# First recurrent step of a fused macaron network: the initial-state products taken out of the gates and added to their biases, and small tables copied by GpSimd

## What is computed

```python
c0 = jnp.broadcast_to(in_c, (batch, in_c.shape[0]))       # one vector, the same for every row
def step(c, xt):                                          # 4 steps over rows of 1024 x 256
    ft = sigmoid(xt @ wf.T + c @ uf.T + bf)
    it = sigmoid(xt @ wi.T + c @ ui.T + bi)
    gt = tanh(xt @ wc.T + c @ uc.T + bc)
    c = ft * c + it * gt
    return (c, None)
c_final, _ = lax.scan(step, c0, x)
h = tanh(einsum('tbi,oi->tbo', x, wo) + c_final @ uo.T + bo)
x = x + 0.5 * h
```

## Time and profile before

| | |
|---|---|
| median of 3 runs | 1934.23 us (1933.54 to 1936.37) |
| the profiled execution's own time | 1933.88 us |
| its span | 1932.1 us |
| TensorE busy | 1752.0 us (91% of the span) |
| VectorE, ScalarE, GpSimd busy | 1340.6, 1130.9, 901.4 us |
| mean granted clock of TensorE | 0.979 of 2.4 GHz |

### The profile page before, as it was taken

The page is one execution under the profiler, slowest core; times in us unless marked ns, Lnnn a source line. Parts: engine busy times, 40 slices in busy tenths (PEclk is TensorE's granted clock), DMA queues, the critical chain, the costliest instruction groups (busy, mean ns, idle before and its releaser), DMA issues. The chain is left out here.

```text
span 1932.1 us, 30828 instructions
## 1 busy us (share of the span) xinstructions
PE 1752.0 (91%) x9742; PEld 1156.5 (60%) x9742; DVE 1340.6 (69%) x2878; ACT 1130.9 (59%) x1624; POOL 901.4 (47%) x654
## 2 busy tenths in 40 slices
PE   5999787999999999997999799997898899989998
PEld 4888673222222222227888677776676676767776
DVE  4545895777777777775555588885677777768886
ACT  3323588999999999994333222213777777622220
POOL 0001116999999999994002232211554445521111
PEclk9999898999999999998999999998999999999999
DMA  4000165534535435300000000001322222300000
GB/s 152 1 0 11 65 186 103 83 44 62 69 43 72 58 46 83 45 1 12 1 0 21 23 17 0 0 0 33 125 89 88 88 88 88 121 2 22 22 21 23
DMA packets 57640, 96.96 MB, mean 50 GB/s; under 512 B 7936, under 2 KB 29664, under 8 KB 57568
## 3 DMA queue, kind: packets, MB, share of 16 engines
q1 hardware_dynamic: 55392, 94.50, 21.7%
q10 hardware_dynamic: 2176, 1.55, 0.2%
HBM read 78.98 MB, written 17.04 MB: 50 GB/s over the span
## 5 line engine op out<-in xcount | busy, mean ns | idle before, releaser
L1232 POOL TENSOR_TENSOR att_weights<-att_weights 128x1024 f32<-128x1024 f32 x288 | 541.0, 1893 | 17.7 <-DVE att_weights L1176 7.3
L1176 DVE SCALAR_TENSOR_TENSOR att_weights<-att_weights,ps 128x512 f32<-128x512 f32 x576 | 370.1, 684 | 152.3 <-ACT att_weights L1152 150.5
L1152 ACT ACTIVATE att_weights<-att_weights 128x1024 f32<-128x1024 f32 x288 | 302.5, 1051 | 0.0
L1148 ACT ACTIVATE att_weights<-ps 128x1024 f32<-128x1024 f32 x288 | 294.1, 1022 | 9.9 <-PE ps L1094 5.6
L720 DVE SCALAR_TENSOR_TENSOR X<-ps,moe_gsel,X 128x256 f32 (+1 forms) x512 | 246.6, 484 | 64.4 <-PE ps L47 48.4
L1108 PE MATMUL ps<-att_weights,att_v_ones 128*32 128x512 f32 (+3 forms) x1536 | 288.8, 497 | 2.6 <-POOL att_weights L1232 2.5
L47 PE MATMUL ps<-w_experts_hi,moe_xh 128*128 128x512 f32 x512 | 205.2, 401 | 0.0
L47 PE MATMUL ps<-w_experts_hi,moe_xl 128*128 128x512 f32 x512 | 203.1, 397 | 0.0
L47 PE MATMUL ps<-w_experts_lo,moe_xh 128*128 128x512 f32 x512 | 201.6, 394 | 0.0
L313 ACT ACTIVATE ffn_gates<-ps,ffn_gate_bias 128x512 f32<-128x512 f32 x96 | 66.1, 688 | 207.2 <-PE ps L47 200.8
L1091 PE MATMUL ps<-q_stack,k_stack 128*128 128x512 bf16 (+3 forms) x384 | 116.8, 341 | 29.5 <-DVE att_weights L1176 19.8
(11 more groups left out here) (257 smaller groups left out, 3881.4 us busy)
## 6 DMA issues: line engine op xcount, KB each, us to landing
ssm_lb<-decays SPq DMA_DIRECT2D x32, 512.0 KB, 4.5
ssm_rise<-decays SPq DMA_DIRECT2D x32, 512.0 KB, 3.8
qk_parts<-qkv_part SPq DMA_DIRECT2D x32, 384.0 KB, 2.6
q_stack<-qk_parts SPq DMA_DIRECT2D x64, 128.0 KB, 4.5
k_stack<-qk_parts SPq DMA_DIRECT2D x64, 128.0 KB, 8.2
att_q_stack<-qk_parts SPq DMA_DIRECT2D x64, 128.0 KB, 4.6
att_k_stack<-qk_parts SPq DMA_DIRECT2D x64, 128.0 KB, 8.0
out<-X SPq DMA_DIRECT2D x8, 512.0 KB, 2.9
```

The costliest lines, as they stand in the source:

```text
L1148: act.activation(Wt[:, u % WU], scores(u), ACT.Exp).then_inc(exp_done, 1)
L1152: act.activation(Wt[:, u % WU], Wt[:, u % WU], ACT.Ln, bias=1.0).then_inc(ln_done, 1)
L1176: dve.scalar_tensor_tensor(out=wt[:, t], in0=wt[:, t], scalar=LIMIT, in1=scores(u)[:, t], op0=ALU.min, op1=ALU.max).then_inc(max_done, 1)
L1232: pool.tensor_tensor(Wt[:, u % WU], Wt[:, u % WU], Wt[:, u % WU], ALU.mult).then_inc(sq_pool, 1)
```

## The change

In the first step of both feed-forward stages the units 0 to 5 hold only W times x, six matmuls instead of twelve. The products U times `in_c` are made once, in the first feed-forward stage, as six columns of PSUM: `start_products(m)` issues for each of three gates four matmuls with one moving column, in full fp32, twelve for each block. VectorE adds the gate biases to the sums (`first_bias`), and ScalarE uses that vector as the bias of its activations in the first step. The second stage uses the same vector again. In the first step the state update is `c = f * in_c + g_in` with `in_c` as a per-partition scalar, one instruction instead of two. `c`, `ch` and `cl` are no longer filled at the start, and the first step is written out ahead of the loop, which now runs over steps 1 and 2. In the first feed-forward stage the matmuls of the identity are gone, and the start products stand on both sides of the first transposes; in the second stage they stay.

In the loading stage, the load of x is issued after three small tables instead of after all nine, and the copies of small tables and the bias subtraction go from VectorE to GpSimd.

```diff
-            norm.pe_first_turn(pe, norm.var_done, ring[:, 0, 0:P], 6, 5)
+            def start_products(m):
+                for gate in range(3):
+                    col = gate * KC + m
+                    for q in range(2 * KC):
+                        part, k = (wh, wl)[q % 2], q // 2
+                        ins = pe.matmul(start_sums[:, col:col + 1], f32(part[:, 3 + gate, k, m * P:(m + 1) * P]),
+                                        in_c[:, k:k + 1], start=q == 0, stop=q == 2 * KC - 1)
+                ins.then_inc(sums_done, 1)
...
-                        matmul3(pe, out, w(wh, gate), w(wl, gate), xh, xl, range(KC), last=False)
-                        pe.wait_ge(c_split, n + 1)
-                        matmul3(pe, out, w(wh, 3 + gate), w(wl, 3 + gate), lambda k: ch[:, h, k, :],
-                                lambda k: cl[:, h, k, :], range(KC), first=False).then_inc(unit_done, 1)
+                        if first:
+                            matmul3(pe, out, w(wh, gate), w(wl, gate), xh, xl, range(KC)).then_inc(unit_done, 1)
+                        else:
+                            matmul3(pe, out, w(wh, gate), w(wl, gate), xh, xl, range(KC), last=False)
+                            pe.wait_ge(c_split, n - 1)
+                            matmul3(pe, out, w(wh, 3 + gate), w(wl, 3 + gate), lambda k: ch[:, h, k, :],
+                                    lambda k: cl[:, h, k, :], range(KC), first=False).then_inc(unit_done, 1)
...
+            if first_of_all:
+                start_products(0)
+                norm.pe_turn(pe, 0, 0)
+                start_products(1)
+            else:
+                norm.pe_first_turn(pe, norm.var_done, ring[:, 0, 0:P], 6, 5)
+            step(0, first=True)
+            with pe.Fori(1, B - 1) as i:
+                step(i)
+            step(B - 1, last=True)
...
         def _(act):
-            for h in range(HALVES):
-                for k in range(KC):
-                    ins = act.activation(c[:, h, k], in_c[:, k:k + 1].broadcast_to([P, GN]), ACT.Copy)
-            ins.then_inc(c_done, 1)
-            for h in range(HALVES):
-                for k in range(KC):
-                    ins = act.activation(ch[:, h, k], in_c[:, k:k + 1].broadcast_to([P, GN]), ACT.Copy)
-            ins.then_inc(ch_done, 1)
...
         def _(dve):
             norm.dve_stats(dve, 0, 0, lambda j: tile_of(0, 0, j))
             norm.dve_apply(dve, 0, 0, lambda j: tile_of(0, 0, j))
-            dve.wait_ge(c_done, 1)
-            dve.wait_ge(ch_done, 1)
-            dve.tensor_tensor(cl[:, :, :, :], c[:, :, :, :], f32(ch[:, :, :, :]), ALU.subtract).then_inc(c_split, 2)
             norm.dve_lo(dve, 0, 0)
+            if first_of_all:
+                dve.wait_ge(sums_done, KC)
+                dve.tensor_tensor(first_bias[:, :], start_sums, gate_bias[:, :], ALU.add).then_inc(first_done, 1)
+
+            def first_update(n, h, m):
+                f, g_in, g = (gates[:, m, q] for q in range(3))
+                dve.wait_ge(unit_read, RING + n * UNITS + 3 * m + 3)
+                dve.tensor_tensor(g_in, g_in, g, ALU.mult).then_inc(ig_done, 1)
+                dve.wait_ge(ig_done, 2 * n + m + 1)
+                dve.scalar_tensor_tensor(out=c[:, h, m], in0=f, scalar=in_c[:, m:m + 1], in1=g_in,
+                                         op0=ALU.mult, op1=ALU.add).then_inc(c_done, 1)
...
         def _(act):
+            for dst, src in smalls[:3]:
+                act.dma_start(dst, src).then_inc(small_in, 16)
+            act.dma_start(x_tiles[:, 0], batches(x_dram)[:, 0]).then_inc(x_in, 16)
+            for dst, src in smalls[3:]:
+                act.dma_start(dst, src).then_inc(small_in, 16)
             act.dma_start(mask[:, :], mask_src).then_inc(small_in, 16)
             act.dma_start(bias_raw[:, :], bias_src).then_inc(small_in, 16)
-            for dst, src in smalls:
-                act.dma_start(dst, src).then_inc(small_in, 16)
-            act.dma_start(x_tiles[:, 0], batches(x_dram)[:, 0]).then_inc(x_in, 16)
...
         def _(dve):
-            dve.wait_ge(small_in, 16 * (len(smalls) + 2))
-            dve.tensor_copy(neg[:, :], mask[:, :]).then_inc(consts_done, 1)
-            dve.tensor_copy(ident16[:, :], smalls[0][0]).then_inc(consts_done, 1)
-            dve.tensor_copy(bias3[:, :], bias_raw[:, :]).then_inc(consts_done, 1)
             split.split_lo(dve)
-            dve.wait_ge(consts_done, 3)
+        def _(pool):
+            pool.wait_ge(small_in, 16 * (len(smalls) + 2))
+            pool.tensor_copy(neg[:, :], mask[:, :])
+            pool.tensor_copy(ident16[:, :], smalls[0][0])
+            pool.tensor_copy(bias3[:, :], bias_raw[:, :]).then_inc(consts_done, 1)
+            pool.wait_ge(consts_done, 1)
             last = slice((TERMS - 1) * ROWS, TERMS * ROWS)
-            dve.tensor_tensor(bias3[last, :], bias_raw[last, :], f32(bias3[last, :]), ALU.subtract).then_inc(consts_done, 1)
-            dve.wait_ge(consts_done, 4)
+            pool.tensor_tensor(bias3[last, :], bias_raw[last, :], f32(bias3[last, :]), ALU.subtract).then_inc(consts_done, 1)
+            pool.wait_ge(consts_done, 2)
```

More of the change, by code:

```diff
@@ L215, in ffn_phase @@
     wh, wl = (part.rearrange("p (m k) c -> p m k c", k=KC) for part in W)
-    gate_bias, in_c, bo_rows = small
+    gate_bias, first_bias, in_c, bo_rows = small
     HALVES = T // GN
     UNITS = 8
+    first_of_all = x_dram is not None
     with Phase(nc) as ctx:
@@ L228, in ffn_phase @@
         ring = ps[:, 2:2 + RING]
+        start_sums = ps[:, 6, 0:3 * KC]
+        sums_done = sem(f"{tag}_sums_done")
+        first_done = sem(f"{tag}_first_done")
         unit_done = sem(f"{tag}_unit_done")
@@ L246, in _, with step @@
         def _(pe):
-            norm.pe_first_turn(pe, norm.var_done, ring[:, 0, 0:P], 6, 5)
-            def step(i, last):
+            def start_products(m):
[6 more added lines that the diff above has]
+                ins.then_inc(sums_done, 1)
+            def step(i, first=False, last=False):
                 for h in range(HALVES):
@@ L303, in _, with step @@
             norm.act_hi(act, 0, 0)
-            def step(i, last):
+            def step(i, first=False, last=False):
+                bias = first_bias if first else gate_bias
                 for h in range(HALVES):
@@ L309, in step @@
                         m, gate = u // 3, u % 3
-                        if u == 0 or u == 3:
-                            act.wait_ge(c_done, 2 * n + 1)
+                        if not first and (u == 0 or u == 3):
+                            act.wait_ge(c_done, 2 * n)
+                        if first and h and (u == 0 or u == 3):
+                            act.wait_ge(c_done, 2)
                         act.wait_ge(unit_done, n * UNITS + u + 1)
                         act.activation(gates[:, m, gate], ring[:, u % RING], ACT.Tanh if gate == 2 else ACT.Sigmoid,
-                                       bias=gate_bias[:, gate * KC + m:gate * KC + m + 1]).then_inc(unit_read, 1)
+                                       bias=bias[:, gate * KC + m:gate * KC + m + 1]).then_inc(unit_read, 1)
                         if u == 4 and not (last and h == HALVES - 1):
@@ L320, in step @@
                                        ring[:, u % RING], ACT.Copy).then_inc(unit_read, 1)
-            with act.Fori(0, B - 1) as i:
-                step(i, False)
-            step(B - 1, True)
+            if first_of_all:
+                act.wait_ge(first_done, 1)
+            step(0, first=True)
+            with act.Fori(1, B - 1) as i:
+                step(i)
+            step(B - 1, last=True)
         @block.vector
@@ L341, in update, with step @@
                 dve.wait_ge(ig_done, 2 * n + m + 1)
-                dve.wait_ge(fc_done, 2 * n + m + 1)
+                dve.wait_ge(fc_done, 2 * (n - HALVES) + m + 1)
                 dve.tensor_tensor(c[:, h, m], f, g_in, ALU.add).then_inc(c_done, 1)
-            def step(i, last):
+            def step(i, first=False, last=False):
+                update = first_update if first else later_update
                 for h in range(HALVES):
@@ L358, in step @@
                     update(n, h, 1)
-                    dve.wait_ge(c_done, 2 * n + 3)
-                    dve.wait_ge(unit_done, n * UNITS + 6)
+                    dve.wait_ge(c_done, 2 * n + 2)
+                    if not first:
+                        dve.wait_ge(unit_done, n * UNITS + 6)
                     dve.tensor_copy(ch[:, h], c[:, h]).then_inc(ch_done, 1)
-                    dve.wait_ge(ch_done, n + 2)
+                    dve.wait_ge(ch_done, n + 1)
                     dve.tensor_tensor(cl[:, h], c[:, h], f32(ch[:, h]), ALU.subtract).then_inc(c_split, 1)
-            with dve.Fori(0, B - 1) as i:
-                step(i, False)
-            step(B - 1, True)
+            step(0, first=True)
+            with dve.Fori(1, B - 1) as i:
+                step(i)
+            step(B - 1, last=True)
             for u in range(PT // 2):
```

14 lines of the change are left out of this document (7 added, 7 removed).

## The result

| | before | after |
|---|---|---|
| median (4 runs each) | 1935.3 us | 1904.66 us |
| profiled execution, its own time | 1933.88 us | 1904.48 us |
| span | 1932.1 us | 1902.7 us |
| TensorE busy | 1752.0 us | 1727.0 us |

The ratio is 0.9848 with a 95% interval of 0.9834 to 0.9862. The forecast was 1901.3 us with a range of 1897 to 1907: the time lies inside it, 3.4 us over the forecast. It lies outside the 1899 to 1904 to which the prediction gave 56.5%, and inside the 1903.8 to 1907 of its rival "cold start", which had 14%.

What follows compares the result with a forecast made beforehand. TensorE was taken to bound the first feed-forward stage's first half. From 1933.88 us, 31.0 (gates), 0.35 (start) and 1.5 (loading) gave 1901.0; the median, 0.35 above the profiled execution, 1901.3 us; range 1897 to 1907.

Steps and rivals of the forecast that it cites:

- cold start: Rival: TensorE's clock is at 1.2 GHz when the first units come; 1903.8 to 1907 us; chance 14%.
- gates of the first step: Both feed-forward stages: six matmuls fewer per unit save 16.8 us less a 1.3 us stall, 31.0 us for both.
- start of the first stage: First feed-forward stage, up to the first unit: start products instead of identity matmuls, a gain of 0.35 us in the sum.
- S + 9.3: Sign, S being the first feed-forward stage's start: a first unit later than this, in us, would make the prediction wrong.
- gate matmuls with a spacing of 0.43 us: Sign that would make the prediction wrong; the spacing read before the change was 0.233 us.
- the chain: First step, from half 2's preceding transposes through activation, state update and statistics to normalisation: 13.4 us against TensorE's 12.2.
- single gate buffer: First step: ScalarE's added wait on the updates of the half before, said to hide with a microsecond to spare.
- x from row 1024 on: Rows 1024 to 2047 wanted at about 43 us, their loads issued by 30.2 us; the wait was said to hide.
- Filling c, ch, cl: Start of both feed-forward stages: eight ScalarE copies and a VectorE subtraction go; their removal is worth nothing.
- Loading: Loading stage: low parts no longer wait for the last small table; ends at 16.6 us, gain 1.5 us, ends 0 and 3.0.
- the feared loss of the whole gain: Loading stage: by the shared read port GpSimd's 1.65 us would add to VectorE's, leaving a gain near 0.
- last rival: Slower: stalls keep TensorE at 1.2 GHz through the first step, 48.8 us more against 32.9 saved; 1950 us; chance 1.5%.

Runs made afterwards that it cites:

- the run with the late split: Changed kernel, but VectorE makes the high and low part of half 0's state after the normalisation of half 2; ratio 0.9845, median 1907.75 us.

## Why the prediction was right, and where it was wrong

The large term, the gates of the first step, was right. The rest of the total was partly luck: the start of the first stage went wrong by 4.4 us, which by the prediction's own signs (a first unit later than S + 9.3, gate matmuls with a spacing of 0.43 us) makes it wrong there, and what happened is its rival "cold start". Stages that nobody touched gave 2.4 us back, and without them the time would have been about 1907, the edge of the range.

- **Gates of the first step: right, mechanism and size.** 16.8 less a stall of 1.3 was forecast. The first step's two halves took 12.15 and 13.29 us in the second stage, 25.4 instead of 41.0: 15.6 us. In the first stage the run without start products shows the same, 25.5 instead of 41.1. The stall was 1.1 us, the chain 13.3 us of 13.4, and moving two instructions out of it removed the stall. The waits that were costed at nothing (single gate buffer, x from row 1024 on) did not show.
- **Filling c, ch, cl: right.** The low part followed the high part at once as before.
- **Start of the first stage: the step that failed.** The sum had a gain of 0.35 us there, and it was a loss of 4.1 us or a little more: the first unit came 2.5 us later than in the kernel before, and the slow matmuls behind it made the first half 1.8 us longer. The failing sentence is "the fast pace came about 4.3 us after the first of them": it carried a row of 128-column matmuls over to matmuls of one column. At the slow pace a record cost 0.214 us, near the 0.227 assumed; at the fast one 0.111, cheaper than the 0.133 assumed. What was wrong is which pace holds. The case "cold start" had it, priced at up to 5.5 us (3.4 for the late first unit, 2.1 behind it) and given 14%; block 1 ended at S + 11.9 instead of 12.7.
- **By the Trainium skill's load time**, 0.107 us for 128 columns in "TensorE: Matmul & The Clock Gate", section "LDWEIGHTS (loading the stationary operand)", a record would cost 0.107; the trace agrees at full speed (0.111) and differs at the low level, where it is 0.214. The page gives one figure for both.
- **Loading: mis-sized, 1.0 instead of 1.5 us.** The place was right: GpSimd's tables ended the stage, and took 2.2 us instead of 1.65. In the changed kernel's own profile the gain was 0.8 us. The first of the tables took 0.76 us while VectorE made its last low part, and 0.37 in the run with the late split, where VectorE was nearly done. In all nine profiles with GpSimd's version this copy took 0.29 to 0.82 us, the longer the more of it lay beside VectorE's last low part, and it ended 0.15 to 0.18 us after it. That agrees with the Trainium skill's "GPSIMD Engine Reference", section "Architecture", by which the two share a read port; it was GpSimd's copy that grew, VectorE's own 0.69 us did not, and the feared loss of the whole gain did not come.
- **What paid it back: luck, as far as the runs show.** The 1.8 us from the attention stages and 0.6 from the rest are no effect that any run ties to the change. In the second profile of the kernel before, attention took 711.1 us, and 709.5 to 710.7 in the profiles of the changed forms. Whether the 0.4 us or more that lie between these groups belong to the change is left open.
- **A slip in the last rival.** "About 33 us spent at the low level" is 33 us of work at full speed; at half the clock it takes 66 us to lose the 32.9 that were saved. The rival did not come, so nothing hangs on it.

## What to carry to other kernels

When matmuls ahead of a dense stretch are replaced, ask what they did for the clock, not only what they computed: here matmuls with 1 or 64 moving columns took as long per record as with 128 at the same level, 0.214 us, and left TensorE at 1.2 GHz, so widening their moving operand to a full tile cost nothing and brought the speed back. A price from a row holds for the shape of that row alone; if the shape changes by a factor of 128, carry both paces as cases. After TensorE's work in a loop is halved, look for instructions in the next chain that nobody needs yet, and let them follow those that somebody waits for.

## What the runs showed of the hardware

- Under fp32 matmuls with 1 or 64 moving columns, back to back but for the transposes between them, TensorE stayed at 1.2 GHz in the whole start of the stage, 11.9 us; with 1 column and 2.4 GHz when they began, it fell to 1.2 under them (0.111, then 0.214 us a record). With 128 columns in the same places it was at 2.4 GHz when block 1 began (0.112 us a record), and where it was at 2.4 GHz from the start, it stayed there, over idle waits of 1.00 and 1.81 us.
- An fp32 matmul of 128 weight columns and 1 moving column shows as two records of 0.111 us each at full speed and 0.214 us at the lower level. The matmul with 128 moving columns cost the same 0.214 at the lower and 0.112 at the higher level.
- The same code after the same idle wait (3.8 us at the second stage's start, 2.1 us ahead of its last products) met the lower level earlier or later: the first transposes took 1.94 or 1.12 us, the last products 1.5 us more or not. That moves a feed-forward stage by 1 to 2 us from run to run, as much as many an edit is worth.
- GpSimd's copy of 128x128 elements took 0.29 us alone and up to 0.82 beside a VectorE subtraction of two SBUF operands, whose 0.69 us stayed as they were.
